# Moving the first group's output projection and norm into the attention loop of a language-model tower

## The chip, the cores and the metric

One Trainium2 chip, one of its cores. The metric is the device time of one launch in microseconds (us), as the median of several runs. The core has a matrix engine (TensorE, PE in the rows, with its weight loads as PEld), VectorE (DVE), ScalarE (ACT), GpSimd (POOL) and SyncE (SP), which here only starts transfers. Each engine runs its own instructions in order and waits on semaphores for the others.

## What the reference computes

The tower has a token encoder of four layers (`L0_tok`), and after it a cross-covariance attention, an expert layer, a full attention and a second expert layer. The change touches the four layers of the token encoder alone. 8 sequences of 256 tokens with 192 features are 2048 tokens, and a layer is, in short:

```python
q = heads(h @ Wq[l] + bq[l]); k = heads(h @ Wk[l] + bk[l]); v = heads(h @ Wv[l] + bv[l])
a = band_attention(q, k, v, mask)          # 12 heads of 16, each token sees 64 to either side
h = layer_norm(h + a @ Wo[l] + bo[l], ln1_s[l], ln1_b[l])
f = gelu(h @ W1[l] + b1[l])                # 192 -> 768
h = layer_norm(h + f @ W2[l] + b2[l], ln2_s[l], ln2_b[l])
```

## The kernel before

The 2048 tokens are 16 tiles of 128 (`NT`), in 4 groups of 4 tiles (`GT`). The body of `Fori(0, L)` is one layer and runs four times; each engine's body is written out by hand, and its order is the order of the code. A layer has these stages.

*First tiles and projections.* The layer's input `h` is turned tile by tile. To turn a tile takes three engines: TensorE transposes it in two 128x128 halves into a bank of PSUM (`pe_transpose`, L364), ScalarE copies the bank to `xx` (`act_split`, L569), and VectorE computes from the bank and the copy what rounding lost (`dve_split`, two instructions, L654 and L655). Then the query, key and value projections of the first group and part of the second are made.

*The attention loop* (`pe_attention`, `act_attention`, `dve_attention`). It goes over 96 pairs of heads (`PAIRS`): 8 sequences, 2 query tiles each, 6 pairs. Step p of an engine's loop holds work of several pairs. TensorE makes the scores of pair p (L469, L472), the values of pair p-5 (L501 to L503) and the transposes of pair p-3 (L483). ScalarE takes two exponentials (L604) and makes the half-precision copy of pair p-3 (L615). VectorE takes the maximum of pair p (L682), and the rest that the copy lost of pair p-4 (L688); every six pairs it also finishes one tile of the attention's output, into `xn` (`dve_finish`, L702 to L715). The remaining projections are strewn over the steps up to p = 67, every third step, into bank 3, which is free after that. GpSimd meanwhile splits projections and weights (L883 is the last instruction of a weight split). VectorE's loop runs 8 steps longer than the pairs, TensorE's 5 and ScalarE's 3.

*The tail.* After the loop come, in this order for groups 0 and 1: turn the group's attention output (`pe_turn`, k = 1), multiply it by the output weights (`pe_out_group`, five matmuls a tile, L392 to L396, into banks 0 and 1), add the residual (`dve_residual`, L753), statistics (`dve_stats`, L762 and L766), the power on GpSimd (`pool_rstd`) and the affine part (`dve_affine`, L796 to L805), which writes the normed `h`. The second group is turned before the first group's affine part. Then the first group's normed `h` is turned (k = 2), and the hidden layers begin (`pe_hidden`, L382 to L386 and L562), in which the later groups' turning, output projection and norm are interleaved by the tables `under` and `TURNED`. `TURNED` and `NORMED` are the orders in which groups are turned and normed; semaphore counts are worked out from them.

Of the kernel before, what the change touches and what calls it, by code (L numbers as in the profile page):

```python
# [24 lines left out]
ALU = mybir.AluOpType  # L25
# [6 lines left out]
P = 128  # L32
# [16 lines left out]
ROWS = DH * len(SLOTS)  # L49
ITEMS = 7  # L50
AHEAD = 3
TURNED = ((1, 0), (1, 1), (2, 0), (2, 1), (1, 2), (2, 2), (1, 3), (2, 3))
NORMED = ((1, 0), (1, 1), (1, 2), (2, 0), (1, 3), (2, 1), (2, 2), (2, 3))
XC_H, XC_D = 8, 24
# [60 lines left out]
def build_tower(nc, a, out, stop=None):  # L115
    ctx = ExitStack()
    with ctx:
# [233 lines left out]
        def turned(k, t):  # L351

            return NT + GT * TURNED.index((k, t // GT)) + t % GT

# [1 line left out]

            return GT * NORMED.index((k, t // GT)) + t % GT + 1

        def pe_transpose(pe, it, s, t, src, ready, turn, n):

            pe.wait_ge(ready.sem, ready.at(turn, n))
            pe.wait_ge(xx_ready.sem, xx_ready.at(it, s - 1))
            for c in range(2):
                last = nc.tensor.transpose(bank[BX[t % 2]][:, c * P:c * P + P],  # L364
                                           src[:, t, c * P:c * P + P], ident[:, :])
            last.then_inc(xt_done.sem, 1)

# [135 lines left out]
                    last = nc.tensor.matmul(o2, ptl[:, p % 2, w], v[:, 0:32], start=False, stop=(c == 1))  # L503
            last.then_inc(pv_done.sem, 1)

        def pe_attention(pe, it, banded, w, before):

            for n in range(ITEMS + AHEAD):
                if n == ITEMS:
                    pe.wait_ge(xx_ready.sem, xx_ready.at(*before["xx"](2 * GT)))  # L510
                pe_qkv(pe, it, n // ITEMS, n % ITEMS, w)
                if n in before:
                    before[n]()
            pe.wait_ge(xx_ready.sem, xx_ready.at(*before["xx"](NT)))
            for p in range(PAIRS + 5):
                if p < PAIRS:
                    pe_scores(pe, it, p, banded)
                if p >= 5:
                    pe_values(pe, it, p - 5)
                if p == 3:  # L520
                    pe.wait_ge(qf_ready.sem, qf_ready.at(it, 3 + AHEAD))
                    pe.wait_ge(vf_ready.sem, vf_ready.at(it, 4))
                if 0 <= p - 3 < PAIRS:
                    pe_turn_probs(pe, it, p - 3)
                if next_projection(p):
                    g, i = next_projection(p)
                    pe_qkv(pe, it, g, i, w)

        def pe_out(pe, it, w, c0, g, xt):

# [33 lines left out]
                    last.then_inc(y_done.sem, 1)  # L564


        def act_split(act, it, s, t):
            act.wait_ge(xt_done.sem, xt_done.at(it, s + 1))
            nc.scalar.activation(xx[:, 0:2, t * P:t * P + P],  # L569
                                 bank[BX[t % 2]][:, 0:2 * P].rearrange("p (a n) -> p a n", a=2),  # L570
                                 ACT.Copy).then_inc(xh_ready.sem, 1)

        def act_turn(act, it, k, g):
# [43 lines left out]
        def act_attention(act, it, banded, split):  # L617

            for n in range(ITEMS + AHEAD):
                if n % ITEMS < 3:  # L620
                    act_qk(act, it, n // ITEMS, n % ITEMS)
                if n in split:
                    split[n]()
            for p in range(PAIRS + 3):
                if p < PAIRS:
                    act_exp(act, it, 2 * p, banded)
                if 0 <= p - 3 < PAIRS:
                    act_hi(act, it, p - 3)
                if p < PAIRS:
                    act_exp(act, it, 2 * p + 1, banded)  # L630
                if next_projection(p):
                    g, i = next_projection(p)
                    if i < 3:
                        act_qk(act, it, g, i)

        def act_hidden(act, it, b1, sigs, func, before):
            u_done, f_ready, y_done, y_read = sigs
# [10 lines left out]
            for t in range(GT * g, GT * g + GT):  # L648
                dve_split(dve, it, turned(k, t), t)

        def dve_split(dve, it, s, t):
            dve.wait_ge(xh_ready.sem, xh_ready.at(it, s + 1))
            ps, tk = bank[BX[t % 2]], slice(t * P, t * P + P)
# [64 lines left out]
        def dve_attention(dve, ch, it, banded, split):  # L718

            for n in range(ITEMS + AHEAD):  # L720
                if n < 3:
                    dve_pieces(dve, ch, it, n)
                elif n < ITEMS:
                    dve_v(dve, it, 0, n - 3, banded)
                if n in split:
                    split[n]()
            for p in range(PAIRS + 8):
                if p < PAIRS:
                    dve_max(dve, it, p, banded)
                if 0 <= p - 4 < PAIRS:  # L730
                    dve_lo(dve, it, p - 4)
                if p and next_projection(p - 1):
                    g, i = next_projection(p - 1)
                    if i >= 3:
                        dve_v(dve, it, g, i - 3, banded)
                if p >= 11 and (p - 11) % 6 < 3 and (p - 11) // 6 < NT:
                    dve_finish(dve, ch, it, (p - 11) // 6, (p - 11) % 6, banded)

# [17 lines left out]
        def dve_stats(dve, ch, it, half, g, read):  # L756

            c = []
            for i in range(GT):
                if read:  # L760
                    dve.wait_ge(read.sem, read.at(it, GT * g + i + 1))
                c.append(ch.mark(nc.vector.bn_stats(stats[:, GT * g + i, :], h[:, GT * g + i, 0:D])))  # L762
            for i in range(GT):
                ch.done(c[i])
                alone(dve)
                last = nc.vector.bn_aggr(mv[:, GT * g + i, :], stats[:, GT * g + i, :])  # L766
                if i < GT - 1:
                    ch.mark(last)
            last.then_inc(mv_ready.sem, 1)
# [39 lines left out]
        def dve_tail(dve, ch, it):  # L809

            first = lambda g: NORMED.index((1, g)) + 1
            second = lambda g: NORMED.index((2, g)) + 1

            def out(g):
                dve_turn(dve, it, 1, g)
                dve_residual(dve, ch, it, 0, g)
                dve_stats(dve, ch, it, 0, g, o_read)

            out(0)
            dve_turn(dve, it, 1, 1)  # L820
            dve_affine(dve, ch, it, first(0), 0, 0)
            dve_residual(dve, ch, it, 0, 1)
            dve_stats(dve, ch, it, 0, 1, o_read)
            dve_turn(dve, it, 2, 0)
            for g in range(NG + 1):
                if g + 1 < NG:
                    dve_affine(dve, ch, it, first(g + 1), g + 1, 0)
                if g:
                    dve_residual(dve, ch, it, 1, g - 1)
                    dve_stats(dve, ch, it, 1, g - 1, y_read)  # L830
                if g + 1 < NG:
                    dve_turn(dve, it, 2, g + 1)
# [765 lines left out]
        def _(act):  # L1598
# [3 lines left out]
            with act.Fori(0, L) as it:  # L1602
                for t in range(GT):
                    act_split(act, it, t, t)
                act_attention(act, it, True, beside(lambda t: act_split(act, it, t, t)))
                for k, g in ((1, 0), (1, 1), (2, 0)):
                    act_turn(act, it, k, g)
                act_hidden(act, it, b1[0], tok_hidden, ACT.Gelu, under(lambda k, g: act_turn(act, it, k, g)))
            for t in range(NT):
                act_split(act, L, t, t)  # L1610
# [42 lines left out]
        def _(dve):  # L1653
# [38 lines left out]
            with dve.Fori(0, L) as it:  # L1692
                ch.enter(it, 512)
                for t in range(GT):
                    dve_split(dve, it, t, t)
                dve_attention(dve, ch, it, True, beside(lambda t: dve_split(dve, it, t, t)))
                dve.wait_ge(rows_y.sem, rows_y.at(it, 16 * 8))
                dve_tail(dve, ch, it)
                ch.round_up()
            ch.leave(L)  # L1700
# [67 lines left out]
        def _(pe):  # L1768
# [6 lines left out]
            with pe.Fori(0, L) as it:  # L1775
# [4 lines left out]
                    first_turn(t)  # L1780
                pe.wait_ge(wa_ready.sem, wa_ready.at(it, 1))
                pe.wait_ge(xx_ready.sem, xx_ready.at(it, GT))
                pe_attention(pe, it, True, wa, beside(first_turn, lambda n: (it, n)))
                pe.wait_ge(wb_ready.sem, wb_ready.at(it, 1))
                pe_turn(pe, it, 1, 0, None)
                pe_out_group(pe, it, wb, 0)
                pe_turn(pe, it, 1, 1, 4)
                pe_out_group(pe, it, wb, 1)
                pe_turn(pe, it, 2, 0, 8)
                pe_hidden(pe, it, wb, w2[0], tok_hidden,  # L1790
# [176 lines left out]
```

## Time and profile before

| what | value |
|---|---|
| time, 3 runs | 2115.87 us median (2114.82 to 2119.48) |
| the profiled execution | 2105.01 us, of which 2103.2 us lie between its first and last instruction (its span) |
| mean granted TensorE clock | 0.876 of full speed |
| TensorE, VectorE, ScalarE, GpSimd busy | 75%, 65%, 53%, 34% of the span |
| first layer: last value matmul of the loop to first hidden matmul | 248.17 us to 272.11 us |

The busy shares are means over very different stages. The profiled execution is 10.9 us shorter than the median of the timed ones, so a sum made against it is a difference, to be taken from either. A start time is in us from the span's start. The durations of neighbouring instructions on one engine can overlap by some 0.1 us, so that what an instruction costs in a row of them is the distance between two starts.

### The profile page before, as it was taken

What the parts mean: (1) busy time and instruction counts of PE and PEld (TensorE: products, weight loads), DVE (VectorE), ACT (ScalarE), POOL (GpSimd) and SP (SyncE); (2) the same over time, 40 slices, a digit from 0 to 9 for tenths busy, and PEclk for the clock granted to TensorE, in tenths of its full rate; (3) what the DMA queues carried; (4) which work ended last, traced back from release to release, by engine and by line L of the source; (5) the groups of instructions that cost most, each with busy time, mean ns of one, the idle gap of its engine ahead of it and who ended that gap; (6) DMA issues with size and microseconds to landing.
All of it is one profiled execution on the core that took longest, in us unless ns stands there. A gap on an engine that the chain in (4) does not pass through costs nothing.

```text
span 2103.2 us, 47757 instructions
## 1 busy us (share of the span) xinstructions
PE 1575.0 (75%) x14634; PEld 1320.4 (63%) x14634; DVE 1356.9 (65%) x3622; ACT 1109.5 (53%) x3351; POOL 717.1 (34%) x989
## 2 busy tenths in 40 slices
PE   0588777798787798786898783875945887649993
PEld 0477666576576676675676672754944666449993
DVE  4688865688765789665888655243436998544444
ACT  0499632698523799323898221323524997225651
POOL 5644123534122542133541231012544340025551
PEclk9999889899798899798999795877976999669996
DMA  5868000875000955003864000004746580137875
GB/s 133 167 111 101 16 1 2 152 96 83 1 1 25 155 80 72 1 2 52 136 96 49 1 1 12 1 21 143 239 126 91 83 100 2 40 120 239 242 233 167
DMA packets 191388, 178.63 MB, mean 85 GB/s; under 512 B 23056, under 2 KB 176208, under 8 KB 190992
## 3 DMA queue, kind: packets, MB, share of 16 engines
q1 hardware_dynamic: 183824, 158.19, 38.4%
q0 software_dynamic: 7296, 17.18, 2.5%
q8 instruction: 130, 2.13, 0.5%
q14 instruction: 138, 1.13, 0.2%
HBM read 132.96 MB, written 42.34 MB: 83 GB/s over the span
## 4 chain that ended last, share of the span: by engine, by line
PE 48%; DVE 24%; issue 12%; ACT 6%; DMA 4%; POOL 3%; SPq 1%; DVEq 1%; ACTq 0%; POOLq 0%
DVE ptl L688 7%; PE bank L1261 6%; PE bank L483 5%; PE bank L562 4%; ACT pth L615 3%; PE bank L501 2%; PE bank L364 2%; DVE neg_max L682 2%; ACT prob L604 2%; PE bank L1247 2%; PE bank L382 2%; DVE h L805 2%; DMA kx<-qk_rows 1%; PE bank L472 1%; PE bank L386 1%
## 5 line engine op out<-in xcount | busy, mean ns | idle before, releaser
L604 ACT ACTIVATE prob<-bank,neg_max 128x192 f32<-128x192 f32 (+1 forms) x960 | 417.1, 440 | 67.5 <-DVE neg_max L682 32.2
L688 DVE TENSOR_TENSOR ptl<-bank,pth 128x512 f16<-128x512 f32 x480 | 329.3, 686 | 34.7 <-ACT pth L615 26.6
L682 DVE TENSOR_REDUCE neg_max<-bank 128x2 f32<-128x384 f32 (+1 forms) x480 | 273.6, 570 | 92.9 <-PE bank L472 90.3
L483 PE MATMUL bank<-ident,prob 128*128 128x128 f32 x1920 | 310.0, 285 | 0.0
L615 ACT ACTIVATE pth<-bank 128x512 f16<-128x512 f32 x480 | 286.9, 598 | 6.4 <-PE bank L483 6.4
L569 ACT ACTIVATE xx<-bank 128x256 fp32r<-128x256 f32 x256 | 94.2, 384 | 365.8 <-PE bank L364 360.0
L501 PE MATMUL bank<-v,pth 128*128 128x32 bf16 x1920 | 199.4, 180 | 107.1 <-DVE ptl L688 94.0
L501 PEld LDWEIGHTS bank<-v,pth 128*128 128x128 f16 x1920 | 154.0, 96 | 197.6 <-DVE ptl L688 187.4
L483 PEld LDWEIGHTS bank<-ident,prob 128*128 128x128 f32 x1920 | 205.6, 143 | 0.2
L604 ACT ACTIVATION_READ_ACCUMULATOR prob<-bank,neg_max 128x1 f32 x960 | 202.6, 211 | 0.0
L503 PE MATMUL bank<-v,ptl 128*128 128x32 bf16 x1920 | 193.6, 176 | 0.0
L502 PE MATMUL bank<-v,pth 128*128 128x16 bf16 x1920 | 190.1, 169 | 0.0
L843 POOL TENSOR_SCALAR rstd<-mv 128x4 f32<-128x4 f32 x52 | 12.0, 231 | 491.0 <-DVE mv L766 485.0
L472 PE MATMUL bank<-kx,qx 96*128 96x192 bf16 (+1 forms) x960 | 169.9, 259 | 7.5 <-DMA kx<-qk_rows 5.3
L364 PE MATMUL bank<-ident,h 128*128 128x128 f32 x256 | 58.6, 352 | 141.2 <-DVE xx L655 88.7
L502 PEld LDWEIGHTS bank<-v,pth 128*128 128x128 f16 x1920 | 157.0, 97 | 0.2
L503 PEld LDWEIGHTS bank<-v,ptl 128*128 128x128 f16 x1920 | 154.7, 96 | 0.0
L643 ACT ACTIVATE fbuf<-bank,b 128x512 f32<-128x512 f32 x96 | 65.9, 687 | 164.7 <-PE bank L386 164.7
L364 PE MATMUL bank<-ident,xn 128*128 128x128 f32 x256 | 62.2, 372 | 117.5 <-DVE xx L655 63.1
L469 PE MATMUL bank<-mask,ident 128*128 128x384 bf16 x384 | 130.4, 340 | 23.6 <-DMA kx<-qk_rows 23.6
L562 PE MATMUL bank<-w,fbuf 128*128 128x192 f32 x768 | 143.0, 332 | 0.0
L562 PEld LDWEIGHTS bank<-w,fbuf 128*128 128x128 f32 x768 | 133.7, 195 | 8.3
(273 smaller groups left out, 4250.0 us busy)
## 6 DMA issues: line engine op xcount, KB each, us to landing
xn<-in_e_seg SPq DMA_DIRECT2D x34, 768.0 KB, 6.8
qx<-qk_rows SPq DMA_DIRECT2D x240, 96.0 KB, 5.0
kx<-qk_rows SPq DMA_DIRECT2D x240, 96.0 KB, 7.2
qk_rows<-fbuf SPq DMA_DIRECT2D x80, 192.0 KB, 2.8
w<-in_e_w SPq DMA_DIRECT2D x23, 576.0 KB, 4.6
qk_rows<-piece_c SPq DMA_DIRECT2D x40, 192.0 KB, 3.0
hb<-in_e_w SPq DMA_DIRECT2D x11, 576.0 KB, 4.3
y_rows<-mask SPq DMA_DIRECT2D x8, 768.0 KB, 8.7
```

What stands on the lines that cost most here:

```text
L364: last = nc.tensor.transpose(bank[BX[t % 2]][:, c * P:c * P + P], src[:, t, c * P:c * P + P], ident[:, :])
L469: nc.tensor.matmul(o, ident_bf, mask[:, 2 * b + qt, :].unsqueeze(1).to_broadcast([P, 2, D]), start=True, stop=False)
L472: last = nc.tensor.matmul(o[:, e, :], qx[0:ROWS, b % 3, hd + e, qt * P:qt * P + P], kx[0:ROWS, b % 3, hd + e, ks], start=not banded, stop= ...
L483: last = nc.tensor.transpose(bank[BT[p % 2]][:, (2 * e + c) * P:(2 * e + c) * P + P], prob[:, qt, hd % PROBS, c * P:c * P + P], ident[:, :])
L501: nc.tensor.matmul(o2, pth[:, p % 3, w], v[:, 0:32], start=(c == 0), stop=False)
L502: nc.tensor.matmul(o1, pth[:, p % 3, w], v[:, 32:48], start=False, stop=False)
L503: last = nc.tensor.matmul(o2, ptl[:, p % 2, w], v[:, 0:32], start=False, stop=(c == 1))
L562: last = nc.tensor.matmul(bank[BY[t]][:, 0:D], fbuf[:, (n - 2) % 4, t * P:t * P + P], w2[:, c, :], start=(c == 0), stop=(c == FC - 1))
L604: nc.scalar.activation(prob[:, qt, hd % PROBS, c0:c0 + n], scores_at(u // 2, n)[:, u % 2, :], ACT.Exp, bias=neg_max[:, tile_no % 3, hd:hd ...
L615: nc.scalar.activation(pth[:, p % 3, :], bank[BT[p % 2]][:, :], ACT.Copy).then_inc(hi_ready.sem, 1)
L682: nc.vector.tensor_reduce(neg_max[:, t % 3, hd:hd + 2], scores_at(p, D if banded else S), AX.X, ALU.max, negate=True).then_inc(max_ready.s ...
L688: nc.vector.tensor_tensor(ptl[:, p % 2, :], bank[BT[p % 2]][:, :], pth[:, p % 3, :], ALU.subtract)\
```

## The change

A new constant `LATE = 70` says where the late work begins. In TensorE's loop step p = 70, 72, ... 92, one of twelve pieces is done at the end of the step: four steps turn tiles 0 to 3 of the attention's output, four make the output projection of these tiles, and four turn tiles 4 to 7. All of them use bank 3 (`BM[0]`) and no second bank, and each waits until the one before it has been read. ScalarE copies the turned tile at the end of its step p, and VectorE splits it, or adds the residual, in its step p + 1. VectorE takes the first group's statistics in step 88 and its affine part in step 98, before it makes the last pair's rest in step 99. The statistics of group 0 move to the last four places of `stats`, since the loop uses the first twelve for its row sums. After the loop, the first group's turning, projection, residual, statistics and affine part and the second group's turning are gone; the second group's projection follows directly. The wait on `rows_y` (weights and norm rows of the layer) moves from the loop's end to step 98 on VectorE, and `wb_ready` to step 78 on TensorE. The attention of the later stage (`banded` false) is as before. The core of the diff:

```diff
+        def late_step(p):
+            i = (p - LATE) // 2
+            if p < LATE or (p - LATE) % 2 or i >= 3 * GT:
+                return None
+            return ("att", i) if i < GT else ("out", i - GT) if i < 2 * GT else ("att", i - GT)
+
+        def pe_late(pe, it, p, w):
+            if late_step(p) is None:
+                return
+            kind, t = late_step(p)
+            if kind == "att":
+                if t == 0:
+                    pe.wait_ge(vf_ready.sem, vf_ready.at(it, 4 * NG))
+                if t == GT:
+                    pe.wait_ge(o_read.sem, o_read.at(it, GT))
+                pe_transpose(pe, it, turned(1, t), t, xn, att_ready, it, t + 1, True)
+            else:
+                if t == 0:
+                    pe.wait_ge(wb_ready.sem, wb_ready.at(it, 1))
+                    pe.wait_ge(xx_ready.sem, xx_ready.at(it, turned(1, GT - 1) + 1))
+                else:
+                    pe.wait_ge(o_read.sem, o_read.at(it, t))
+                pe_tokens(bank[BM[0]][:, 0:D], w, 0, D, t).then_inc(o_done.sem, 1)
...
+        def dve_late(dve, ch, it, p):
+            if late_step(p - 1):
+                kind, t = late_step(p - 1)
+                if kind == "att":
+                    dve_split(dve, it, turned(1, t), t, True)
+                else:
+                    dve.wait_ge(hb_ready.sem, hb_ready.at(it, normed(2, t) - 2 * NT))
+                    dve.wait_ge(o_done.sem, o_done.at(it, t + 1))
+                    nc.vector.tensor_tensor(h[:, t, 0:D], bank[BM[0]][:, 0:D], hb[:, t, :], ALU.add)\
+                        .then_inc(o_read.sem, 1)
+            if p == LATE + 4 * GT + 2:
+                dve_stats(dve, ch, it, 0, 0, o_read)
+            if p == PAIRS + 2:
+                dve.wait_ge(rows_y.sem, rows_y.at(it, 16 * 8))
+                dve_affine(dve, ch, it, NORMED.index((1, 0)) + 1, 0, 0)
...
@@ in pe_attention, at the end of a step
+                if late:
+                    pe_late(pe, it, p, late)
@@ in act_attention, at the end of a step
+                if banded and late_step(p) and late_step(p)[0] == "att":
+                    act_split(act, it, turned(1, late_step(p)[1]), late_step(p)[1], True)
@@ in dve_attention, after the maximum, the rest and a value projection, before dve_finish
+                if banded:
+                    dve_late(dve, ch, it, p)
@@ in dve_tail
-            out(0)
-            dve_turn(dve, it, 1, 1)
-            dve_affine(dve, ch, it, first(0), 0, 0)
             dve_residual(dve, ch, it, 0, 1)
             dve_stats(dve, ch, it, 0, 1, o_read)
             dve_turn(dve, it, 2, 0)
@@ scalar
-                for k, g in ((1, 0), (1, 1), (2, 0)):
-                    act_turn(act, it, k, g)
+                act_turn(act, it, 2, 0)
@@ vector
-                dve.wait_ge(rows_y.sem, rows_y.at(it, 16 * 8))
@@ tensor
-                pe_attention(pe, it, True, wa, beside(first_turn, lambda n: (it, n)))
-                pe.wait_ge(wb_ready.sem, wb_ready.at(it, 1))
-                pe_turn(pe, it, 1, 0, None)
-                pe_out_group(pe, it, wb, 0)
-                pe_turn(pe, it, 1, 1, 4)
+                pe_attention(pe, it, True, wa, beside(first_turn, lambda n: (it, n)), wb)
                 pe_out_group(pe, it, wb, 1)
                 pe_turn(pe, it, 2, 0, 8)
```

## Rows read from the trace of the kernel before

**Rows 1.** Page: parts 1 and 2 (VectorE's busy time; granted TensorE clock, 40 slices)

```profile
PE 1575.0 (75%) x14634; PEld 1320.4 (63%) x14634; DVE 1356.9 (65%) x3622; ACT 1109.5 (53%) x3351; POOL 717.1 (34%) x989
...
PEclk9999889899798899798999795877976999669996
```

**Rows 2.** Busy time by stretch: start:end, length, then per engine busy (x instructions); clock; DMA

```profile
226.58:235.23 8.65, 7.39 (x114) 5.88 (x115) 7.98 (x19) 8.08 (x32) 0.00 (x0) 1.00 0.01 2
...
189.68:199.11 9.43, 8.45 (x124) 7.09 (x124) 8.46 (x20) 8.42 (x32) 3.66 (x9) 1.00 0.91 118
...
179.82:189.68 9.86, 8.93 (x124) 7.25 (x124) 8.90 (x19) 9.16 (x33) 6.33 (x9) 1.00 0.28 68
...
249.00:275.00 26.00, 18.30 (x69) 13.91 (x68) 18.52 (x72) 4.81 (x13) 5.43 (x9) 0.50 0.00 1
```

**Rows 3.** Waits, 205 to 237 us: who waited for whom, total us, times, longest

```profile
PEld bank L501 <- DVE ptl L688: 8.8, 17, 1.8
```

**Rows 4.** TensorE in order of time: start, length (us), line, tiles, idle before and releaser

```profile
248.17 0.19 PE L503 MATMUL bank<-v,ptl 128*128 128x32 bf16 x1
...
252.10 0.53 PE L392 MATMUL bank<-wb_hi,xx 128*128 128x192 f32 x1 [0.60 <-DVE xx L655]
...
253.28 0.41 PE L392 MATMUL bank<-wb_hi,xx 128*128 128x192 f32 x1
...
272.11 0.79 PE L382 MATMUL bank<-xx,wb_hi 128*128 128x512 f32 x1 [1.13 <-DVE xx L655]
...
288.32 0.39 PE L392 MATMUL bank<-wb_hi,xx 128*128 128x192 f32 x1
...
288.99 0.28 PE L392 MATMUL bank<-wb_hi,xx 128*128 128x192 f32 x1
...
852.43 0.19 PE L503 MATMUL bank<-v,ptl 128*128 128x32 bf16 x1
...
876.38 0.79 PE L382 MATMUL bank<-xx,wb_hi 128*128 128x512 f32 x1 [1.13 <-DVE xx L655]
```

**Rows 5.** VectorE in order of time, end of the first layer's loop and tail

```profile
245.86 0.69 DVE L688 TENSOR_TENSOR ptl<-bank,pth 128x512 f16<-128x512 f32 x1 [0.59 <-ACT pth L615]
...
247.11 0.69 DVE L688 TENSOR_TENSOR ptl<-bank,pth 128x512 f16<-128x512 f32 x1 [0.56 <-PE bank L503]
...
248.49 0.23 DVE L702 SCALAR_TENSOR_TENSOR rs<-stats,pad_keys 128x12 f32<-128x12 f32 x1 [0.68 <-PE bank L503]
...
249.76 0.28 DVE L654 TENSOR_TENSOR xx<-bank,xx 128x128 fp32r<-128x128 f32 x1
...
250.22 0.28 DVE L654 TENSOR_TENSOR xx<-bank,xx 128x128 fp32r<-128x128 f32 x1
...
253.59 0.36 DVE L753 TENSOR_TENSOR h<-bank,hb 128x192 f32<-128x192 f32 x1 [1.09 <-PE bank L396]
...
256.79 0.36 DVE L753 TENSOR_TENSOR h<-bank,hb 128x192 f32<-128x192 f32 x1 [0.71 <-PE bank L396]
...
258.44 0.29 DVE L654 TENSOR_TENSOR xx<-bank,xx 128x128 fp32r<-128x128 f32 x1
...
261.15 1.40 DVE L796 SCALAR_TENSOR_TENSOR hb<-h,mv,ln_s 128x192 f32<-128x192 f32 x4
...
264.56 0.61 DVE L753 TENSOR_TENSOR h<-bank,hb 128x192 f32<-128x192 f32 x2
...
269.24 0.29 DVE L654 TENSOR_TENSOR xx<-bank,xx 128x128 fp32r<-128x128 f32 x1
```

**Rows 6.** GpSimd beside VectorE at 218 us, its power, and ScalarE's copy of turned tiles

```profile
218.08 1.52 POOL L883 TENSOR_TENSOR wa_second_lo<-raw,wa_second 64x576 fp32r<-64x576 f32 x1
...
218.25 1.43 DVE L715 TENSOR_TENSOR xn<-au,rs 128x64 f32<-128x64 f32 x1
...
259.13 1.04 POOL L844 TENSOR_TENSOR rstd<-rstd,neg_half 128x4 f32<-128x4 f32 x1 [0.18 <-POOL rstd L843]
...
277.16 0.66 ACT L569 ACTIVATE xx<-bank 128x256 fp32r<-128x256 f32 x2
```

More of the change, by code:

```diff
@@ L51 @@
 AHEAD = 3
+LATE = 70
 TURNED = ((1, 0), (1, 1), (2, 0), (2, 1), (1, 2), (2, 2), (1, 3), (2, 3))
@@ L357, in normed, with turn_at, pe_transpose @@
             return GT * NORMED.index((k, t // GT)) + t % GT + 1
-        def pe_transpose(pe, it, s, t, src, ready, turn, n):
+        def turn_at(t, inside):
+            return bank[BM[0] if inside else BX[t % 2]]
+        def late_step(p):
[20 more added lines that the diff above has]
+                pe_tokens(bank[BM[0]][:, 0:D], w, 0, D, t).then_inc(o_done.sem, 1)
+        def pe_transpose(pe, it, s, t, src, ready, turn, n, inside=False):
             pe.wait_ge(ready.sem, ready.at(turn, n))
-            pe.wait_ge(xx_ready.sem, xx_ready.at(it, s - 1))
+            pe.wait_ge(xx_ready.sem, xx_ready.at(it, s if inside else s - 1))
+            o = turn_at(t, inside)
             for c in range(2):
-                last = nc.tensor.transpose(bank[BX[t % 2]][:, c * P:c * P + P],
+                last = nc.tensor.transpose(o[:, c * P:c * P + P],
                                            src[:, t, c * P:c * P + P], ident[:, :])
@@ L504, in pe_values, with pe_attention @@
             last.then_inc(pv_done.sem, 1)
-        def pe_attention(pe, it, banded, w, before):
+        def pe_attention(pe, it, banded, w, before, late=None):
             for n in range(ITEMS + AHEAD):
@@ L564, in pe_hidden, with act_split @@
                     last.then_inc(y_done.sem, 1)
-        def act_split(act, it, s, t):
+        def act_split(act, it, s, t, inside=False):
             act.wait_ge(xt_done.sem, xt_done.at(it, s + 1))
             nc.scalar.activation(xx[:, 0:2, t * P:t * P + P],
-                                 bank[BX[t % 2]][:, 0:2 * P].rearrange("p (a n) -> p a n", a=2),
+                                 turn_at(t, inside)[:, 0:2 * P].rearrange("p (a n) -> p a n", a=2),
                                  ACT.Copy).then_inc(xh_ready.sem, 1)
@@ L649, in dve_turn, with dve_split @@
                 dve_split(dve, it, turned(k, t), t)
-        def dve_split(dve, it, s, t):
+        def dve_late(dve, ch, it, p):
[13 more added lines that the diff above has]
+                dve_affine(dve, ch, it, NORMED.index((1, 0)) + 1, 0, 0)
+        def dve_split(dve, it, s, t, inside=False):
             dve.wait_ge(xh_ready.sem, xh_ready.at(it, s + 1))
-            ps, tk = bank[BX[t % 2]], slice(t * P, t * P + P)
+            ps, tk = turn_at(t, inside), slice(t * P, t * P + P)
             nc.vector.tensor_tensor(xx[:, 2, tk], ps[:, 0:P], xx[:, 0, tk].bitcast(F32), ALU.subtract)
@@ L761, in dve_stats @@
                     dve.wait_ge(read.sem, read.at(it, GT * g + i + 1))
-                c.append(ch.mark(nc.vector.bn_stats(stats[:, GT * g + i, :], h[:, GT * g + i, 0:D])))
+                c.append(ch.mark(nc.vector.bn_stats(stats[:, (GT * g + i + NT - GT) % NT, :], h[:, GT * g + i, 0:D])))
             for i in range(GT):
@@ L765, in dve_stats @@
                 alone(dve)
-                last = nc.vector.bn_aggr(mv[:, GT * g + i, :], stats[:, GT * g + i, :])
+                last = nc.vector.bn_aggr(mv[:, GT * g + i, :], stats[:, (GT * g + i + NT - GT) % NT, :])
                 if i < GT - 1:
```

## Prediction

> **What bounds the kernel now.** I read the page first, for the spread of the load. No engine is busy for the whole span, so a mean share decides nothing, and the clock line shows slices at six and seven tenths beside slices at nine [rows 1]. So I asked for busy times by stretch, around the place that the change touches. The loop's last quarter and the tail behind it are two regimes. Six pairs of the loop that carry nothing but attention take 8.65 us, and in them ScalarE is busy for 8.08 us and VectorE for 7.98 us, with TensorE's clock at 1.00. The 26 us behind the loop show VectorE busy for 18.52, ScalarE for 4.81, and the clock at 0.50, which is the 1.2 GHz level [rows 2]. The reader is to see that the loop is nearly full on two engines, and that the tail is a chain in which everybody waits in turn.
>
> The waits of the loop say how it is held together: TensorE's weight loads for the values wait 17 times for VectorE's rest L688, 8.8 us in 32 [rows 3]. So ScalarE's and VectorE's work, with 0.57 and 0.67 us free in 8.65, sets the pace, and TensorE has room. Then I read the tail in order of time on TensorE and on VectorE. The last value matmul of the first layer ends at 248.17 + 0.19 = 248.36 us and the first hidden matmul starts at 272.11: 23.75 us. In the third layer it is 876.38 - 852.62 = 23.76 us [rows 4]. I take 23.75 us a layer, four times.
>
> **What is left behind the loop.** I rebuild the new tail from pieces of the old one, counted from the end of the last value matmul.
> - To the second group's projection: it starts at once, since its tiles are turned by then. Tiles follow one another in 253.28 - 252.10 = 1.18 and then 1.07 us at the low clock.
> - VectorE first finishes the last attention tile: from 248.49 to 249.76 it takes 1.27 us, 1.40 us after the matmul's end [rows 5]. The first residual of a group comes 253.59 - 252.10 = 1.49 us after its matmul starts, so the finish costs nothing there.
> - Residuals and statistics: from the group's first matmul (252.10) to the first split after its statistics (258.44) are 6.34 us [rows 4, 5]. The same will follow the new loop.
> - Turning the normed first group: the first split at 269.24, the first hidden matmul at 272.11: 2.87 us [rows 4, 5].
> The tail becomes 6.34 + 2.87 = 9.2 us at the low clock. Removed are then 23.75 - 9.2 = 14.5 us a layer. At full clock a tile's five matmuls take 288.99 - 288.32 = 0.67 us for the first and about half the low clock's time for the others [rows 4], and the tail would be nearer to 7 us; the clock fell with the end of the loop before, and the new loop ends with a pause, so I take 9.2 and keep 7 for the range.
>
> **The pause at the loop's end.** The affine part now stands in step 98, between the rests of the last two pairs. It is 4 + 8 instructions, 261.15 to 264.56: 3.41 us. The rest of pair 94 ends near 246.5 (the row at 245.86), and that of pair 95 started at 247.11 [rows 5]. With 3.4 us between them it starts at 249.9: 2.8 us later. Behind it, on TensorE, stand the values of pair 95, and the whole second group's projection. Only 0.6 us of the affine part is hidden, in VectorE's wait of 0.56 us. The power on GpSimd, which the affine part waits for, was started after step 88 and is long done.
>
> **What the loop takes on.** Twelve pieces and the statistics, in steps 70 to 93.
> - Four output projections. TensorE has five matmuls each, about 0.6 us, and VectorE one addition of 0.36 us. The loop has the same pair of operations earlier, in the value projections: the stretch 189.68 to 199.11 holds two of them in six pairs and takes 9.43 us where the bare one takes 8.65: 0.39 us each [rows 2]. Four: 1.6 us.
> - Eight turned tiles. TensorE has two transposes, ScalarE one copy (two in 0.66 us, so 0.33) [rows 6], VectorE two instructions at a distance of 250.22 - 249.76 = 0.46 us [rows 5]. There is no such step in the loop, so I bound it. If the copy and split fit in the idle 0.57 and 0.67 us of six pairs, three of them cost about 1.0 - 0.6 = 0.4 us on ScalarE, 0.15 each. If each pays VectorE's full 0.46 it is 0.46. Three in six pairs bring VectorE to 7.98 + 1.4 = 9.4 us busy and ScalarE to 9.1; with the 0.5 to 0.7 us of idle time that such six pairs kept so far, that is 9.9 to 10 us, or 0.43 each. The stretch 179.82 to 189.68, which has one query-key projection and one value projection, has ScalarE at 9.16 busy in 9.86 us [rows 2]: the idle time does stay at about 0.7. I take 0.43, eight times: 3.4 us.
> - The statistics: from the last residual 256.79 to the first split 258.44 are 1.65 us, of which 1.3 belong to them [rows 5]. They fall among the turned tiles, where VectorE has nothing left. I take 1.0 (bounds 0.3 and 1.4).
> The loop grows by 1.6 + 3.4 + 1.0 = 6.0 us a layer. The low bound is 8 x 0.15 + 4 x 0.3 + 0.3 = 2.7; the high one is every piece at the sum of its VectorE time and as much again in waits, some 10.
>
> Costed at nothing are three things. The wait for the single bank 3: TensorE takes a piece at the end of step p and the next at the end of p + 2, while VectorE reads it in step p + 1; in between TensorE itself must wait for VectorE's rest of step p + 1, so the bank is read by then; without that cover it would be an exposed 0.46 us and two hand-overs each. The moved waits: the weights of the layer were loaded and split long before step 78. No transfer is added or moved. Last, GpSimd: while its L883 ran from 218.08 for 1.52 us, VectorE's L715 took 1.43 us where it otherwise takes 0.22, and ends with it [rows 6]. That hiccup is in the time already. The new copies and splits read PSUM, and new work of this kind beside GpSimd is only its power instruction, 1.04 us, once a layer [rows 6].
>
> The Trainium skill (SBUF — State Buffer, section "SBUF: two separate sides") says that a VectorE operation with two SBUF inputs is blocked for the whole time of a GpSimd operation that reads SBUF. The trace agrees at 218 us (1.43 us for 0.22). By that rule the late splits and residuals, each with one input in PSUM, stay free beside the weight split, and only a finish instruction could be caught by the power: 4 x 1 us at most, and the sum would be 19 us of gain in place of 23.
>
> **The sum.** A layer: 23.75 - 9.2 - 2.8 - 6.0 = 5.75 us less. Four layers: 23 us. The profiled execution would go from 2105.0 to 2082, and the median of the runs, 10.9 us above it, from 2115.9 to 2093 us. The hidden layers behind start in the same order with the same queues, so nothing of the gain should be given back there, up to where in them the clock rises: before, it rose about 3 us after their start.
>
> **The rivals.**
> - *The loop swallows the pieces, and the clock stays up.* The engines' idle time is used up and the loop grows by 2.7 us only; the tail takes 7 us. For it: TensorE has 1.26 us free in six bare pairs. Against: ScalarE has 0.57. Gain 23.75 - 7 - 2.8 - 2.7 = 11.2 us a layer, 45 us in all: 2071. If only one of the two holds, it is 2080 to 2084.
> - *The hand-overs are exposed* (the other side). Each piece goes TensorE, ScalarE, VectorE and back through one bank, with in-order engines; if an engine reaches its piece before the other is done, it waits with the whole loop behind it, and the delay goes round. A turned tile is then about 0.6 + 0.4 + 0.5 = 1.5 us, a projection 1.0, the loop grows by 8 x 1.5 + 4 x 1.0 + 1.4 = 17 us, and a layer is 17 + 2.8 + 9.2 - 23.75 = 5.6 us slower: 2138. It decides against the change from 11.7 us of growth on, or 1 us a piece. Against it: value projections, with the same kind of hand-over, cost 0.39.
> - *The work is only moved.* What VectorE does in the loop costs in full and with it some waiting, growth 11 to 12 us: within 4 us of before.
>
> **How the numbers follow.** The forecast, a growth of 3 to 9 us and a gain of 12 to 36 us, gets 0.68. The first rival (more than 36 us) gets 0.12, a small gain of 4 to 12 us 0.08, the third rival 0.05, the second 0.07. A measurement of this kernel tells about 0.2%, 4.2 us, from no change. So faster has 0.88, the same 0.05, slower 0.07. The range leaves out the first rival's far end and all that is slower: 2074 to 2107 us, which is a gain of 42 to 9 us.
>
> **What would show it.** In the profile of the changed kernel: the time from the last value matmul to the first hidden matmul at 9 us (7 if the clock is at 1.00 there); VectorE's L796 to L805 between the last two L688, and a gap of some 3 us on TensorE before the last values; six pairs with turned tiles at about 9.9 us and with projections at 9.8; and L364, L569 and L654 inside the loop without waits of over 0.3 us. I am wrong if TensorE waits for L655 or L753 within the loop, or if the idle time of VectorE and ScalarE there grows instead of shrinking.

## Result and profile after

| | before | changed |
|---|---|---|
| time, median | 2117.68 us (2114.82 to 2121.51, 4 runs) | 2084.4 us (2081.12 to 2086.87, 4 runs) |
| ratio | | 0.9847, 95% interval 0.9824 to 0.987 |
| profiled execution | 2105.01 us | 2083.07 us |

The ratio is a gain of 32 us, between 27.5 and 37.3. Predicted were 23, in a range of 9 to 42. The gain is 1.5% of the whole time, since the change touches four layers of a longer program. Two further measurements of the changed kernel, on other chips, gave 0.9841 (0.9818 to 0.9864) and 0.984 (0.9813 to 0.9867).

Page, parts 1 and 2 of the changed kernel, which answer to [rows 1]:

```profile
PE 1567.8 (75%) x14634; PEld 1321.3 (63%) x14634; DVE 1350.8 (65%) x3622; ACT 1106.3 (53%) x3351; POOL 710.9 (34%) x989
...
PEclk9899888899898999898998885877967999669996
```

The work is the same in number (14634 matmuls, 3622 VectorE instructions); it lies closer. The loop's end and the tail of the third layer, TensorE and VectorE in order of time [rows 4, 5]. L741 is the rest L688 of before, L851 to L860 the affine part L796 to L805, L533 to L535 the values, L424 the output projection, L414 the first hidden matmul:

```profile
841.23 0.69 DVE L741 TENSOR_TENSOR ptl<-bank,pth 128x512 f16<-128x512 f32 x1 [0.19 <-ACT pth L649]
841.83 1.40 DVE L851 SCALAR_TENSOR_TENSOR hb<-h,mv,ln_s 128x192 f32<-128x192 f32 x4
...
844.98 0.35 DVE L860 SCALAR_TENSOR_TENSOR h<-hb,rstd,ln_b 128x128 f32<-128x128 f32 x1
845.25 0.69 DVE L741 TENSOR_TENSOR ptl<-bank,pth 128x512 f16<-128x512 f32 x1
...
847.89 0.35 DVE L808 TENSOR_TENSOR h<-bank,hb 128x192 f32<-128x192 f32 x1
...
851.00 0.36 DVE L808 TENSOR_TENSOR h<-bank,hb 128x192 f32<-128x192 f32 x1 [0.71 <-PE bank L428]
...
852.65 0.29 DVE L707 TENSOR_TENSOR xx<-bank,xx 128x128 fp32r<-128x128 f32 x1
```

```profile
845.99 0.21 PE L533 MATMUL bank<-v,pth 128*128 128x32 bf16 x1 [3.55 <-DVE ptl L741]
...
846.33 0.51 PE L424 MATMUL bank<-wb_hi,xx 128*128 128x192 f32 x1
...
847.49 0.41 PE L424 MATMUL bank<-wb_hi,xx 128*128 128x192 f32 x1
...
855.53 0.79 PE L414 MATMUL bank<-xx,wb_hi 128*128 128x512 f32 x1 [1.13 <-DVE xx L708]
```

The twelve affine instructions stand between the last two rests, TensorE waits 3.55 us for the second, and the hidden layers start 9.04 us after the last value matmul. The four shorter tails among the twelve of the three profiles of this kernel (8.7 to 8.8 us) go with a mean granted clock of 0.69 or 0.70 in the tail, the others with 0.50. Busy time of the same stretches [rows 2]:

```profile
841.00:847.00 6.00, 2.12 (x38) 1.78 (x35) 5.13 (x17) 0.79 (x2) 0.00 (x0) 0.65 0.02 4
847.00:856.00 9.00, 6.59 (x28) 5.26 (x28) 6.19 (x26) 1.54 (x4) 2.90 (x5) 0.50 0.00 0
```

The rest of the comparison is by four marks in each layer, read from the timelines: the maxima of pairs 70 and 95, the end of the last value matmul, the start of the first hidden matmul. "Loop" is from pair 70 to 95, "pause" from there to the last value, "tail" from there to the hidden layers; us, layers 1 to 4:

| kernel | loop | pause | tail |
|---|---|---|---|
| before | 37.35, 38.76, 37.29, 38.75 | 7.49, 6.89, 6.92, 6.92 | 23.75, 23.50, 23.76, 23.75 |
| changed | 42.79, 41.21, 40.50, 40.93 | 9.86, 9.86, 9.85, 9.85 | 9.03, 8.74, 9.04, 9.04 |

The means give +3.3, +2.8 and -14.7 us: 8.6 us a layer, 34.4 in four. The profiled spans differ by 22 only. Of the missing 12, some 3.5 lie in the hidden layers and in the steps before 70, in both directions by layer, and 9 behind the fourth layer's first hidden matmul: 922.9 us before (2103.2 - 1180.31), 931.8 in the changed kernel.

### The profile page after: what moved, and what is told of

Read it like the earlier page. It is cut to its first block, busy times and chain, and to the rows that moved or that the text cites. A ratio compares the mean times of both kernels' runs of the same rounds, so it can differ in the third digit from the quotient of the medians.

```text
span 2081.2 us, 47737 instructions
## 1 busy us (share of the span) xinstructions
PE 1567.8 (75%) x14634; PEld 1321.3 (63%) x14634; DVE 1350.8 (65%) x3622; ACT 1106.3 (53%) x3351; POOL 710.9 (34%) x989
## 4 chain that ended last, share of the span: by engine, by line
PE 49%; DVE 23%; issue 11%; ACT 6%; DMA 5%; POOL 2%; SPq 2%; DVEq 1%; ACTq 0%; POOLq 0%
PE bank L1313 6%; DVE ptl L741 6%; PE bank L596 5%; PE bank L515 4%; DVE neg_max L735 3%; PE bank L533 2%; PE bank L396 2%; ACT pth L649 2%; DMA kx<-qk_rows 2%; PE bank L414 2%; PE bank L1299 2%; PE bank L504 2%; ACT prob L638 2%; PE bank L417 2%; PE bank L416 2%
## 5 line engine op out<-in xcount | busy, mean ns | idle before, releaser
L741 DVE TENSOR_TENSOR ptl<-bank,pth 128x512 f16<-128x512 f32 x480 | 329.3, 686 | 24.9 <-ACT pth L649 20.5
L533 PE MATMUL bank<-v,pth 128*128 128x32 bf16 x1920 | 199.5, 180 | 114.1 <-DVE ptl L741 99.6
L533 PEld LDWEIGHTS bank<-v,pth 128*128 128x128 f16 x1920 | 154.3, 96 | 200.3 <-DVE ptl L741 193.8
L535 PE MATMUL bank<-v,ptl 128*128 128x32 bf16 x1920 | 193.9, 176 | 1.3 <-issue 1.3
L535 PEld LDWEIGHTS bank<-v,ptl 128*128 128x128 f16 x1920 | 154.7, 96 | 0.0
L396 PE MATMUL bank<-ident,xn 128*128 128x128 f32 x256 | 57.8, 344 | 105.1 <-DVE xn L831 53.4
```

What stands on the lines that cost most here:

```text
L396: last = nc.tensor.transpose(o[:, c * P:c * P + P], src[:, t, c * P:c * P + P], ident[:, :])
L533: nc.tensor.matmul(o2, pth[:, p % 3, w], v[:, 0:32], start=(c == 0), stop=False)
L741: nc.vector.tensor_tensor(ptl[:, p % 2, :], bank[BT[p % 2]][:, :], pth[:, p % 3, :], ALU.subtract)\
```

## Experiments

**Before and changed kernel again.**

> The kernel before, unchanged, for a second profile of it. The profiled execution of before was 10.9 us shorter than the median of the timed ones, while the stages up to the fourth layer's hidden part explain 31 us of difference to the changed kernel and the whole span shows only 22. If the missing 9 us are variation of the later stages (projected cross-covariance attention, experts), this profile has the token layers as before within 1 us each (last value matmul to first hidden matmul 23.5 to 23.8 us in all four), and differs from before behind 1180 us by several us. If the change itself costs 9 us behind the token layers, this profile is within 3 us of before there.

> The changed kernel, unchanged, on this chip beside the others. Theory (the 9 us that the profile showed lost behind the token layers were variation): from the fourth layer's first hidden matmul to the end 921 to 926 us as in the profiles of before and of its repetition (923 and 924), not 932; ratio to before 0.984 to 0.986. The first layer's steps 70 to 78 took 15.95 us where the other layers took 13.6 to 14.1: if that is variation too it is gone here, if it comes with the change it is there again.

> The changed kernel once more, beside the two versions of the spread affine part on one chip, since their ratios to before so far come from different chips. Ratio to before 0.983 to 0.986.

| kernel | loop | pause | tail | last hidden start to end |
|---|---|---|---|---|
| before, again | 38.60, 38.56, 38.06, 38.65 | 7.56, 6.89, 6.89, 6.92 | 23.75, 23.42, 23.75, 23.76 | 923.9 |
| changed, again | 40.22, 40.25, 40.62, 40.37 | 10.32, 9.85, 9.86, 10.33 | 9.03, 8.78, 9.03, 9.04 | 925.1 |
| changed, third | 41.50, 40.65, 40.89, 40.57 | 9.84, 9.85, 9.86, 9.85 | 9.04, 8.78, 9.03, 8.72 | 927.3 |

The second profile of before (923.9 us, within 1 us of the first) spoke by itself for the other reading, that the change costs 9 us there. The profiles that followed decided for variation: the changed kernel has 925.1 and 927.3 there, its variants below 922.0 to 928.3, and a variant of before 926.1. So most of the 9 us is variation; whether 1 or 2 us of it belong to the change can't be told.

The first layer's slow steps 70 to 78 were not there in the second profile (13.39 us for 15.95), and milder in the third (14.55). Three variants of the changed kernel have them in full (15.92, 16.09, 15.92). Two things meet there. TensorE stands for 0.7 to 0.8 us without a wait that the profile shows, 10.6 to 10.7 us after the maximum of pair 70; such a stop is in the kernel before too (1.20 us in the first layer of its second profile, with 12.80 us for 11.88). And in the four profiles with these slow steps, and in no other, TensorE's granted clock falls to 0.50 for 3.4 us right behind the stop; in the third profile the stop is there (1.07 us) and the clock stays at 1.00. VectorE waits 1.82 us for TensorE behind it. What makes TensorE stop was not found.

The timed ratio, 0.984 three times, is the figure to trust, and one profiled execution of this program is good to about 10 us.

**GpSimd's weight split held back**, in the kernel before. The prediction had counted the stop at 218 us [rows 6] as there to stay.

```diff
                 pool.wait_ge(rows_x.sem, rows_x.at(it + 1, 48))
+                pool.wait_ge(pv_done.sem, pv_done.at(it, PAIRS))
```

> The kernel before, with GpSimd's split of the next layer's weights held back until the last value matmul of the loop; nothing else. In before, VectorE's finish of an attention tile ran into GpSimd's two-input subtractions in all four layers: L714 and L715 took 1.4, 1.6, 1.3 and 2.4 us more than elsewhere, 6.7 us in all. Theory (the collision costs the loop in full): the loop's steps 70 to 95 take 35.7 to 36.5 us in every layer instead of 37.3 to 38.8, and the kernel is 5 to 7 us faster. Rival (the collision is covered by other engines' work): within 1 us of before. A third way: the split lands in the tail and delays the statistics' power on GpSimd or VectorE's two-input instructions there, and the tail grows by more than 1 us.

Measured: ratio 0.9949 (0.993 to 0.9967), 11 us faster. Loop 36.52, 36.64, 36.06 and 36.39 us, tail 23.96 and 24.25 three times. The first theory holds for the loop (two layers lie 0.02 and 0.14 us above its range). The timed gain is larger than forecast by 4 to 6 us, which its profile doesn't explain: the marks give 5 to 6 us. VectorE's finish in the loop, and GpSimd's split with VectorE's work beside it in the tail:

```profile
822.92 0.35 DVE L714 TENSOR_TENSOR xn<-au,rs 128x192 f32<-128x192 f32 x1
823.18 0.22 DVE L715 TENSOR_TENSOR xn<-au,rs 128x64 f32<-128x64 f32 x1
```

```profile
852.45 0.66 POOL L880 CAST wa_second<-raw 128x576 fp32r<-128x576 f32 x1
853.29 1.42 POOL L882 TENSOR_TENSOR wa_lo<-raw,wa_hi 128x576 fp32r<-128x576 f32 x1 [0.18 <-POOL wa_second L880]
```

```profile
852.47 0.85 DVE L714 TENSOR_TENSOR xn<-au,rs 128x192 f32<-128x192 f32 x1
...
853.38 0.28 DVE L654 TENSOR_TENSOR xx<-bank,xx 128x128 fp32r<-128x128 f32 x1
853.58 0.33 DVE L655 SCALAR_TENSOR_TENSOR xx<-xx,lo_rows,bank 128x128 fp32r<-128x128 f32 x1
```

In the loop L715 is back at 0.22 us. The half microsecond of longer tail is the same stop in a new place: L714, both inputs in SBUF, takes 0.85 us beside the cast L880. L654 and L655, with one input in PSUM, are not slowed beside L882. So the loop of before had on average 1.6 to 2.1 us a layer (38.04 and 38.47 less 36.40) of this stop. L714 and L715 alone are longer by 1.3 to 2.4 us in each of the eight layers of its two profiles. There L882 and L883 run from 13.1 to 17.5 us after the maximum of pair 70, and L714 starts at 14.3 to 15.2. In the changed kernel the split comes at much the same time (the two subtractions start between 11.9 and 15.8 us), but the same instruction, now L767, starts at 16.0 to 18.5 us, as the late pieces have put it back. Other instructions of the finish are caught now and then:

```profile
217.86 1.41 POOL L934 TENSOR_TENSOR wa_lo<-raw,wa_hi 128x576 fp32r<-128x576 f32 x1 [0.18 <-POOL wa_second L932]
```

```profile
218.14 1.16 DVE L755 SCALAR_TENSOR_TENSOR rs<-stats,pad_keys 128x12 f32<-128x12 f32 x1
```

This one, 0.9 us over its 0.22, is the largest in its first profile; the other layers have 0.6, 0.15 and 0.46, and the second profile 0.3 in all four together. By layer that is 0.5 and 0.1 us, and 0.3 in the third profile, where the two profiles of before have 1.7 and 1.5.

**One part alone**: only the first group is turned in the loop.

```diff
-            if p < LATE or (p - LATE) % 2 or i >= 3 * GT:
+            if p < LATE or (p - LATE) % 2 or i >= GT:
                 return None
-            return ("att", i) if i < GT else ("out", i - GT) if i < 2 * GT else ("att", i - GT)
+            return ("att", i)
@@ everything else behind the loop, in the order of before
```

> One part of the change alone: only the first group's four turned tiles are made in the loop (steps 70 to 76); projection, residual, statistics, affine part and the second group's turning stand behind the loop as before. Theory (0.42 us for a turned tile in the loop against 3.7 us of chain behind it): steps 70 to 78 take 13.5 to 14.1 us as in the changed kernel, the tail 20.0 to 20.3 us instead of 23.75, the pause at the end 6.9 as before; 2 us a layer, 8 us faster than before, and up to 14 if the finish instructions no longer meet GpSimd's subtractions. Rival (the gain is from removing both groups' chains together and a single one is hidden behind the last tile's finish): tail over 22 us and no gain.

Measured: 0.9904 (0.9879 to 0.993), 19 to 20 us faster. That is more than the 8 us, and the up to 14, of the forecast. Loop 39.04, 39.09, 38.17, 39.04, pause 6.88, tail 18.40, 19.74, 19.75, 19.73. By the profile a layer is 38.84 + 6.88 + 19.41 = 65.1 us for 69.2 in the second profile of before, 4.1 less, 16 us in four; the rest is not in these marks. The tail confirms that the chain of a group's turning leaves it whole, a little more because the projection now starts while the clock is still up (in the third layer it is at 1.00 until 1.7 us behind the last value matmul); two tiles follow one another in 0.62 us, for 1.18 in [rows 4]:

```profile
845.83 0.34 PE L424 MATMUL bank<-wb_hi,xx 128*128 128x192 f32 x1
...
846.45 0.27 PE L424 MATMUL bank<-wb_hi,xx 128*128 128x192 f32 x1
```

**The pieces without a free step between them**, in steps 70 to 81.

```diff
-            i = (p - LATE) // 2
-            if p < LATE or (p - LATE) % 2 or i >= 3 * GT:
+            i = p - LATE
+            if p < LATE or i >= 3 * GT:
```

> The changed kernel with the twelve late pieces in twelve steps running (70 to 81) instead of every second one; statistics and affine part where they are. Theory (a piece costs the engines' own work of about 0.4 us wherever it stands, the hand-over through one bank is hidden): steps 70 to 95 within 1 us of the changed kernel's 40.5 to 41.2, same time within 4 us. Rival (the hand-over TensorE, ScalarE, VectorE, TensorE is hidden only by the free step between two pieces): TensorE waits for VectorE's L708 in these steps, a turned tile costs 0.5 us and more on top, 4 to 6 us a layer, 16 to 24 us slower than the changed kernel.

Measured: 1.0088 (1.0056 to 1.012), 19 us slower than before, 52 slower than the changed kernel. Loop 49.07, 54.68, 57.51, 57.50. The theory as written fails. The rival's mechanism is there, at more than its price: the loop is 14 us a layer longer than in the changed kernel's second profile, for a forecast of 4 to 6. Its waits from 200 to 260 us (first layer), then two late splits on VectorE, and the transposes on TensorE behind them:

```profile
PEld bank L396 <- DVE xx L708: 6.9, 6, 1.2
PE bank L396 <- DVE xx L708: 5.5, 6, 0.9
...
PEld bank L424 <- DVE h L696: 2.9, 3, 1.0
```

```profile
206.93 0.34 DVE L708 SCALAR_TENSOR_TENSOR xx<-xx,lo_rows,bank 128x128 fp32r<-128x128 f32 x1
...
209.39 0.34 DVE L708 SCALAR_TENSOR_TENSOR xx<-xx,lo_rows,bank 128x128 fp32r<-128x128 f32 x1
```

```profile
207.32 0.44 PE L396 MATMUL bank<-ident,xn 128*128 128x128 f32 x2 [0.91 <-DVE xx L708]
...
209.79 0.44 PE L396 MATMUL bank<-ident,xn 128*128 128x128 f32 x2 [0.92 <-DVE xx L708]
```

TensorE stands 0.9 us before each transpose with the next scores behind it, a round is 2.47 us for a pair of 1.44. That accounts for the first layer, whose clock stays at 1.00. In the others it falls to 0.50 inside the loop, for 24, 34 and 34 us, from 13.3, 5.9 and 5.9 us after the maximum of pair 70 on. In the fourth layer, against the first (second row):

```profile
1144.00:1166.00 22.00, 20.15 (x172) 16.11 (x172) 12.91 (x33) 12.78 (x45) 0.00 (x0) 0.52 0.01 1
```

```profile
220.00:240.00 20.00, 14.96 (x209) 12.16 (x210) 15.22 (x40) 14.90 (x54) 0.00 (x0) 1.00 0.01 2
```

In the first layer no engine is full (VectorE is busy for 15.22 of 20.00 us), so it is the hand-over that sets the pace, not the amount of work. In the fourth, at the low clock, TensorE is busy for 20.15 of 22.00 us and the others wait for it (waits from 1144 to 1166 us):

```profile
DVE neg_max L735 <- PE bank L504: 9.1, 7, 2.1
ACT prob L638 <- PE bank L515: 7.7, 5, 2.2
...
PEld bank L396 <- DVE xx L708: 2.5, 3, 0.8
```

Why the clock falls in three layers and not in the first is open: up to 5.9 us after pair 70 TensorE is busy for 4.06 us in the first layer and 4.07 in the fourth.

The changed kernel has no wait of TensorE for L708 or L696 among the waits of its third layer's steps 70 to 95; the longest between these engines are of the kind of [rows 3]:

```profile
PEld bank L533 <- DVE ptl L741: 8.2, 19, 1.4
PE bank L533 <- DVE ptl L741: 3.5, 7, 1.2
ACT prob L638 <- DVE neg_max L735: 2.9, 9, 0.6
```

**The affine part elsewhere.** First one step later, behind the last rest:

```diff
-            if p == PAIRS + 2:
+            if p == PAIRS + 3:
```

> The changed kernel with the affine part of group 0 moved one step, behind the last pair's rest (step 99 for 98). Theory (3.4 us of affine part between two rests delay the last values by 2.9 us, and nothing else hangs on its place): from the last maximum to the last value matmul 7.0 us instead of 9.85; the finish of tile 15 and the first residual then come later, tail 10.8 to 11.2 instead of 9.0; net 1 us a layer, 3 to 5 us faster than the changed kernel, 36 us faster than before. Rival (the pause is what keeps the clock low in the tail): the clock stays at 1.00 for the second group's projection and the tail is under 9 us, 10 us faster than the changed kernel.

Measured: 0.981 (0.9783 to 0.9837). Pause 6.92, 6.89, 6.92, 7.57, tail 11.60, 11.63, 11.60, 11.60: what the pause gives back, the tail takes but for 0.1 to 0.4 us (pause and tail are 18.7 us together, and 18.8, 19.1 and 18.7 in the three profiles of the changed kernel). The theory had 1 us. The clock is still low there, 0.50 in three tails and 0.56 in one, so the rival fails too. I had put the tail at 11.2; the residuals came later by the affine part in full. The time is 36.5 us under before's, as forecast, but whether the ratio is better than the changed kernel's can't be told from these intervals.

Then one tile each in steps 96 to 99:

```diff
-            if p == PAIRS + 2:
-                dve.wait_ge(rows_y.sem, rows_y.at(it, 16 * 8))
-                dve_affine(dve, ch, it, NORMED.index((1, 0)) + 1, 0, 0)
+            if PAIRS <= p < PAIRS + GT:
+                if p == PAIRS:
+                    dve.wait_ge(rows_y.sem, rows_y.at(it, 16 * 8))
+                dve_affine(dve, ch, it, NORMED.index((1, 0)) + 1, 0, 0, (p - PAIRS,))
```

> The changed kernel with the affine part of group 0 cut into four tiles, one each in steps 96 to 99, into VectorE's idle time of 0.3 to 0.7 us per step at the loop's end. Theory: last maximum to last value matmul 7.8 to 8.2 us instead of 9.85, tail unchanged at 9.0 (up to 9.3), 1.7 us a layer: 6 to 8 us faster than the changed kernel, about 40 us faster than before. Rival (only the amount of VectorE work counts, not its place): same time as the changed kernel.

> The spread affine part beside the changed kernel. Theory (the pause at the loop's end is 8.7 instead of 9.9 to 10.3 us and the tail 9.16 instead of 9.03): 1.0 to 1.4 us a layer, 4 to 6 us faster than the changed kernel. Rival (the 0.0045 between their ratios was the chips): within 2 us.

Measured: 0.9796 (0.9771 to 0.9821), and beside the changed kernel 0.9791 (0.9766 to 0.9817) against 0.984 (0.9813 to 0.9867): 9 us faster than it in the medians, 2069.94 and 2079.38. The intervals overlap by a little; all five runs of the one lie below all five of the other. Pause 8.69, tail 9.15, in both profiles and all layers. The first forecast had put the pause at 7.8 to 8.2 and missed it; a gain there is. By these two marks it is 0.9 to 1.2 us a layer, 4 to 5 of the 9 us; the rest is not in them, and in the two profiles taken side by side the loop of the spread version is even 0.4 us longer. That the spread version is faster is measured; that the shorter pause is all of it is not shown. No affine tile is followed by a wait on VectorE:

```profile
839.12 0.41 DVE L853 SCALAR_TENSOR_TENSOR hb<-h,mv,ln_s 128x192 f32<-128x192 f32 x1
839.57 0.35 DVE L859 SCALAR_TENSOR_TENSOR h<-hb,rstd,ln_b 128x128 f32<-128x128 f32 x1
839.84 0.35 DVE L862 SCALAR_TENSOR_TENSOR h<-hb,rstd,ln_b 128x128 f32<-128x128 f32 x1
840.10 0.68 DVE L742 TENSOR_TENSOR ptl<-bank,pth 128x512 f16<-128x512 f32 x1
```

With the weight split held back as well, between the two powers:

> The changed kernel with the affine part spread over steps 96 to 99 and GpSimd's weight split held back until the last value matmul, between the powers of the first and the second group. Theory (the two gains add, less 0.5 us of longer tail as in the kernel before): steps 70 to 95 at 40.0 us in every layer, pause 8.7, tail 9.2 to 9.7; 2 to 4 us faster than the spread alone, ratio to before 0.977 to 0.979. Rival (the second group's power now waits for the weight split, which takes 4.3 us from the loop's end on, and the next stage waits for it): tail over 10.5 us and slower than the spread alone.

Measured: 0.9804 (0.9777 to 0.9831), loop 40.34, 41.18, 40.33, 40.24, tail 9.52. Theory and rival both fail in their times. The loop is 0.4 to 0.8 us shorter than with the spread alone (40.52 in the mean, for 40.95 and 41.33), the tail 0.4 us longer, and the ratio no better than the 0.9796 and 0.9791 of the spread alone. And with the statistics cut up too, one tile each in steps 86, 88, 90 and 92:

> As the spread affine part, and the statistics of group 0 also one tile each in steps 86, 88, 90 and 92 instead of all four in step 88. Theory (a burst of 1.4 us on VectorE stops TensorE and ScalarE, and four pieces of 0.35 us fall partly into idle time; each step pays one wait for its own result more): steps 86 to 94 take 12.7 to 13.1 us instead of 13.4, 1 to 3 us faster than the spread alone. Rival (these steps are full on VectorE, so only the sum counts, and the added waits are extra): 13.4 us or more, not faster.

Measured: 0.9826 (0.98 to 0.9852), steps 86 to 94 take 13.93 us where the burst takes 13.5 in the mean. The rival holds: on the same chip it is 6.7 us slower than the spread alone, 2 us of which are in the loop's marks. Each tile has now a wait of its own (0.15 us before the aggregate, and the next instruction later):

```profile
825.86 0.35 DVE L702 BATCH_NORM_STATS2 stats<-h 128x6 f32<-128x192 f32 x1
826.36 0.18 DVE L704 BATCH_NORM_AGGREGATE mv<-stats 128x2 f32<-128x6 f32 x1 [0.15 <-DVE stats L702]
```

## Why the prediction was right, and where its sum was off

The change is faster by the mechanism foretold, by 32 us where 23 were forecast: a chain that waits in turn is taken apart and put into steps that were not full. By the prediction's own steps:
- *What is left behind the loop*, 9.2 us at the low clock: 9.03, 8.74, 9.04, 9.04. The granted clock was 0.50 there in three layers, as taken, and 0.70 in the second. That the tail would take 7 us at 1.00, no run shows.
- *The pause at the loop's end*, 2.8 us: 2.8 in the mean, 3.0 in the repetition. That it sits on the path is borne out by the spread version: 8.69 for 9.85 us, and 9 us faster in the timed runs.
- *What the loop takes on*, 6.0 us: 3.3 in the first pair of profiles, 1.9 in the second. This is the term that was mis-sized, for two reasons. The first is the price of the pieces. Against the loop without the stop, 36.40 us, the changed one takes 40.37 in its least disturbed profile: 4.0, not 6.0 (5.0 and 4.5 in the two others, with the slow first layer and what is left of the stop). Six pairs with three turned tiles (from pair 70) take 9.82 us in that profile for 8.61, 0.40 a tile: the 9.9 us and the 0.43 of the prediction were right. Six pairs with three projections (from pair 78) take 9.33 us for 8.62, 0.24 each for my 0.39, which is 9.33 for my 9.8. Steps 86 to 94, with four turned tiles and the statistics, grow from 11.30 to 13.42, 2.1 us for my 2.7; how that divides between the two isn't measured. I had taken the projection's price from a value projection, which has GpSimd's pieces beside it; that this makes the difference is not shown.
- *"That hiccup is in the time already"*: it was, and I took it to remain. Most of it went, 1.1 us a layer in the first pair of profiles and 1.4 in the second by the lengths of the instructions caught, and that is the other part. The row was on the table; the step I failed to make was to ask whether the slower loop would still be at the same instruction when the split arrives. These 4 to 6 us of the gain are luck: the change was not made for them.
- *Hand-overs costed at nothing*: right, and only because of the free step. Without it twelve pieces cost 13 to 21 us over the 36.40 instead of 4, 13 where the clock stays up. The rival on the other side had 17 us of growth and 2138 us. (Its sum as written, 17 + 2.8 + 9.2 - 23.75, gives 5.25 us a layer; the 5.6 goes with 17.4.) The kernel with the pieces in running steps comes near it, with 16.7 us over before in the mean, but in three layers with the help of a clock that the rival did not have.
- *The rule on two SBUF inputs beside GpSimd*, which the prediction took from the Trainium skill (SBUF — State Buffer, section "SBUF: two separate sides"): this case's rows agree, with 0.85 for 0.35 us beside a cast and 1.16 for 0.22 beside a subtraction, and 0.28 and 0.33, unchanged, with an input in PSUM. The small loss that I drew from it (the power) was not seen; the large effect was the opposite, a loss of before that went away.
- *The first rival* had the loop grow by 2.7 us, the tail take 7 us, and 2080 to 2084 us if only one of the two held. The growth (3.3 and 1.9) is nearer to its 2.7 than to my 6.0, and the 2084.4 measured lies at its edge. The mechanism is only in part its own: VectorE's idle time is used up beside the statistics and halved beside the turned tiles, but 1.6 to 2.1 us of what keeps the growth small is the stop of before, which it did not have.
- *The signs*: no late transpose, copy, split, projection or addition in the loop has idle time before it on its engine that the profile shows, as forecast. One sign of being wrong did come. In six pairs with turned tiles VectorE's idle time falls from 0.67 to 0.30 us, and in six with the statistics from 0.81 to none. But ScalarE's grows, from 0.4 us to between 1.0 and 1.5 beside the projections and from 0.57 to 1.45 beside the statistics. So the pieces do cost waiting on ScalarE; it is VectorE that the late steps fill.

The three terms put in as measured in the two repetitions are 14.7 - 3.0 - 1.9 = 9.8 us a layer, 39 us, in the first pair of profiles 34; the timed gain is 27.5 to 37.3.

## What to carry to other kernels

A tail in which three engines wait in turn can be worth taking into a loop that is 93% full, if each piece gets the steps that its hand-over takes; put into running steps, the same pieces made the kernel slower than it was. Split a long VectorE piece where that engine idles anyway (the loop's last steps), and leave it whole where it doesn't. When a change alters a loop's pace, look for instructions of two engines that stop each other at a fixed meeting point: that cost can vanish or appear.

## What the runs showed of the hardware that was not expected

A VectorE instruction of 0.22 us was held for 1.43 us by one GpSimd subtraction, and two instructions of the finish were thus longer by 1.3 to 2.4 us in each of eight profiled layers; the loop without them was 1.6 to 2.1 us shorter in the mean. GpSimd's cast of 0.66 us does it too (0.85 for 0.35 us). With pieces in running steps TensorE's granted clock fell to 0.50 inside the loop for 24 to 34 us in three layers, where the first layer, with the same instructions, kept 1.00: its loop took 49.07 us and the fourth layer's 57.50. At the low clock it is TensorE that the others wait for (busy 20.15 of 22.00 us). A fall of 3.4 us right behind a stop of TensorE of 0.7 to 0.8 us goes with 1.4 us and more in a first layer's steps 70 to 78 (15.92 to 16.09 us, for 14.55 with the stop alone).
